# Rows of the next stage's input scattered by the two-expert stages, and one block for the start of the 64-wide attention, in an eight-stage kernel

## The chip, the cores and the metric

The kernel runs on one core of one Trainium2 chip. A core has TensorE (PE, matrix products), VectorE (DVE), ScalarE (ACT), GpSimd (POOL) and SyncE (SP, which here only issues DMAs), each with a queue of its own that is worked off in order; they meet through semaphores. DMAs issued by SyncE or GpSimd run on 16 shared DMA engines. The metric is the time of one execution in microseconds on the device; lower is better.

## The reference, cut to what matters

Input is x of 16 × 512 tokens of 128 floats. Eight layers follow, each with a layer norm ahead and a residual sum:

```python
x = x + attn_a(layernorm(x))          # 16 heads of 8, q and k through an rms norm
x = x + pair_ffn(layernorm(x))        # 8 experts, 2 chosen
x = x + attn_b(layernorm(x))          # 16 heads of 8, with a bias that decays with distance
x = x + pair_ffn(layernorm(x))
x = x + attn_relative(layernorm(x))   # 16 heads of 8, relative positions
x = x + choice_ffn(layernorm(x))      # each of 8 experts picks its tokens
x = x + attn_wide(layernorm(x))       # 16 heads of 64, q and k scaled to length 1
x = x + choice_ffn(layernorm(x))
```

The two layers that the change is about, in what they compute:

```python
def pair_ffn(x):                      # x is the normalised input
    gates = sinkhorn((x @ router_w + router_b) / max(temperature, 0.1), 3)
    vals, idx = top_k(gates, 2)
    g = relu(x @ wg[e]);  p = x @ wp[e]          # 128 -> 256, for every expert e
    out_e = (g * p) @ wo[e]                      # 256 -> 128
    return x + sum over the 2 of out_e * vals_e / (sum(vals) + 1e-8)

def attn_wide(x):
    q, k, v = x @ Wq.T, x @ Wk.T, x @ Wv.T       # 128 -> 16 heads of 64
    q = l2norm(q) * q_scale;  k = l2norm(k) * k_scale
    return softmax(q @ k.T / 8) @ v  @ Wo.T + bo
```

So a token leaves a two-expert layer as x + xn + y, with xn the normalised x and y the weighted results of its two experts.

## The kernel before

X, all 8192 tokens, stays in SBUF as [128, 64, 128] floats (4 MB): 16 batches of 512 tokens, four tiles of 128 tokens each. `model()` calls eight stages: narrow_attention ("rms"), pair_feed_forward (top2_a, whose tiles print as `_top_a`), decay_attention ("decay"), pair_feed_forward (top2_b), narrow_attention ("relative"), choice_feed_forward (choice_a), wide_attention ("wide") and choice_feed_forward (choice_b). Every stage consists of one or two blocks; a block has a program for each engine, and no engine enters the next block before all have left this one.

**pair_feed_forward** (L2544). SyncE loads the weights. TensorE turns X and scores it against the router; the normalised tokens `xn` are made in halves: batches 0 to 7 by GpSimd, two instructions of 128x512 each (subtract L2882, multiply L2884), batches 8 to 15 by VectorE, one instruction per tile (L2935, 32 in all). VectorE goes on with the router's chain (L2939 and below), which ends in lists: `from_row`, which token stands in which row of which block, and `to_row`, to which row of the result it goes. There are 91 blocks of 128 rows, each for one pair of experts. SyncE stores `xn` with the token's two gates, 130 floats a token, as `xn_rows` in DRAM (L2687, 4 DMAs). GpSimd then issues all the traffic of the expert loop: `gather(k)` (L2888) reads 128 rows of `xn_rows` into a ring of 12 buffers `xg`, `scatter(k)` (L2894) writes the block's 128 result rows `yg` to `y_rows`; 12 gathers go ahead, then it is scatter, gather, scatter, gather. Rows of a block that belong to no token go to dump rows behind. A block on TensorE is 25 matmuls; VectorE multiplies the halves (`hidden`), copies the higher expert's weights (`bring_higher`) and adds the weighted two results (`both_parts`, L3078) into `yg`. In blocks 12 to 27 VectorE also adds `xn` to X (L3065, 16 instructions of 128x512). After the last scatter SyncE waits until all have landed, reads `y_rows` back in 4 DMAs of 1 MB (L2694), and VectorE adds it to X (L3113, 16 instructions).

**choice_feed_forward** (choice_a) does it otherwise: its scatters accumulate into `x_mid` in DRAM (L3273), and the stage behind loads X from there.

**The attention stages.** In the first stage, "rms", X comes from the input: SyncE issues the first batch's tiles (L591), the setup loads (L593), the second batch's (L595) and the other 14 (L598), and VectorE waits on x_first, x_second and x_rest at its first use of each. The stages decay and relative find X in SBUF; there SyncE issues only setup loads (L1763, L593), and later `no_shift` (L1771, L601), in relative also the bias rows (L604, L608), and then the stores of each batch's q and k parts to scratch (L1844, L662). Before those it clears the semaphores of the stage before.

**wide_attention** (L3541). A first block loads X's tiles and all weights; TensorE transposes 32 squares of 128x128 in eight groups (L3626: groups 0 to 3 are Wq and Wk, 4 and 5 Wv, 6 and 7 Wo), ScalarE copies each group (L3639), and TensorE and ScalarE bring the scales (L3630, L3641). A second block does the attention, whose order is a schedule of steps that every engine walks through. For the first batch it is: layer norm, TURN_X (L3748, transposes of xn), then for t = 0 to 3 QK (L3756, four products of 512 columns, which go through the two banks of `bench`), SQUARES (copy L3843 and square L3846 by ScalarE, sums L3915 by VectorE), ROOT (L3922), LNEXP (L3852, L3854) and NORM (L3930); then seven TURNs (L3774, transposes of q and k, copies by ScalarE). Then come the scores S (L3787), exponentials (L3888), sums (L3936), V (L3764) and the products with v for batch 0, into which the same steps for batch 1 are woven.

## Time and profile before

| | us |
|---|---|
| median of 3 runs | 5938.82 (5938.35 to 5939.02) |
| the profiled execution | 5937.41 |
| its span in the trace | 5935.6 |
| TensorE busy | 4886.7 (82%) |
| VectorE busy | 3676.8 (62%) |
| ScalarE busy | 3305.6 (56%) |
| GpSimd busy | 1501.5 (25%) |

The mean granted clock of TensorE is 0.906 of full speed. The 64-wide attention lies between 3672 and some 5535 us of the trace, the two two-expert stages between 668 and 1103 and between 2081 and 2516. The shares are means over eight stages with different limits; what a stretch is bound by is read from the windows and the order of events in it. Times in the rows are in us from the span's start. A row of the timeline gives start, length, engine and line, output and inputs, shapes and a count, and in brackets the idle time of the engine before it and what ended it.

### The profile page before, as it was taken

How to read it: one execution, taken by the hardware profiler on the slowest of the kernel's cores; microseconds unless marked ns; L12 is line 12 of the kernel's file. 1: busy time of each engine (PE TensorE's matmuls, PEld its weight loads, DVE VectorE, ACT ScalarE, POOL GpSimd, SP SyncE). 2: the span in 40 equal slices, each digit the busy share in tenths (PEclk: the TensorE clock that was granted, in tenths of full speed). 3: DMA queues.
4: the chain of work that ended last, by engine and by line, in shares of the span. 5: the costliest groups of instructions: out<-in, count | busy, mean ns of one | idle time of the engine just before them, and what ended most of it. 6: DMA issues, size and time to landing. Idle time of an engine off the chain costs nothing. (4 is left out here: it accounts for less than half of the span.)

```text
span 5935.6 us, 94648 instructions
## 1 busy us (share of the span) xinstructions
PE 4886.7 (82%) x30116; PEld 2539.8 (43%) x30212; DVE 3676.8 (62%) x7406; ACT 3305.6 (56%) x5224; POOL 1501.5 (25%) x1452
## 2 busy tenths in 40 slices
PE   6999769389888859758888476899999999999557
PEld 2222469334444449712222354343343343343445
DVE  5444564577777785467777761667667666666671
ACT  5999525345555515448888022656666656666113
POOL 1111137324334217623322175000000000000157
PEclk8999779689999959979999577999999999999678
DMA  3222122313333221223222224000000000000213
GB/s 81 64 64 64 40 53 50 81 54 89 88 96 92 74 52 48 68 60 66 58 55 49 66 45 78 1 0 0 0 0 0 0 0 0 0 0 0 66 30 49
DMA packets 227987, 264.41 MB, mean 45 GB/s; under 512 B 36842, under 2 KB 194378, under 8 KB 221320
## 3 DMA queue, kind: packets, MB, share of 16 engines
q1 hardware_dynamic: 184276, 194.33, 12.5%
q0 software_dynamic: 43392, 66.05, 6.2%
q8 instruction: 173, 2.83, 0.2%
q14 instruction: 146, 1.20, 0.1%
HBM read 163.33 MB, written 96.12 MB: 44 GB/s over the span
## 5 line engine op out<-in xcount | busy, mean ns | idle before, releaser
L3888 ACT ACTIVATE prob_wide<-slot_wide 128x1024 f32<-128x1024 f32 x512 | 494.0, 1016 | 149.7 <-PE slot_wide L3787 149.7
L2172 ACT ACTIVATE prob_decay<-slot_decay 128x640 f32<-128x640 f32 x512 | 359.0, 706 | 342.6 <-PE slot_decay L2019 341.5
L996 ACT ACTIVATE prob_rms<-slot_rms 128x1024 f32<-128x1024 f32 x512 | 503.7, 1088 | 57.6 <-PE slot_rms L839 55.4
L2506 DVE TENSOR_TENSOR slot_decay<-slot_decay,dtab_decay 128x512 f32<-128x512 f32 (+3 forms) x1024 | 454.1, 493 | 128.6 <-PE slot_decay L1998 101.8
L996 ACT ACTIVATE prob_relative<-slot_relative 128x1024 f32<-128x1024 f32 x512 | 497.6, 1046 | 48.0 <-PE slot_relative L839 46.5
L3787 PE MATMUL slot_wide<-qT_wide,kT_wide 64*128 64x512 f32 x2048 | 508.8, 615 | 2.9 <-ACT prob_wide L3888 2.9
L3253 POOL TENSOR_TENSOR xn_choice_b<-X,stats_choice_b 128x512 f32<-128x512 f32 x8 | 8.4, 1047 | 1892.6 <-DVEq L3435 1892.6
L1361 DVE TENSOR_TENSOR prob_relative<-prob_relative,rtab_relative 128x1024 f32<-128x1024 f32 (+1 forms) x256 | 394.3, 1546 | 130.8 <-ACT prob_relative L996 122.7
L3800 PE MATMUL obank_wide<-prob_wide,v_wide 128*64 128x512 f32 x2048 | 467.7, 598 | 1.8 <-DVE zT_wide L3950 1.8
L3936 DVE TENSOR_TENSOR sums_wide<-sums_wide,prob_wide 128x1024 f32<-128x1024 f32 x256 | 313.6, 1225 | 28.7 <-ACT prob_wide L3888 0.2
L863 PE MATMUL obank_relative<-prob_relative,vaug_relative 128*32 128x512 f32 x2048 | 276.2, 612 | 39.5 <-DVE prob_relative L1361 38.0
L3861 ACT ACTIVATE rinv_wide<-rbank_wide 128x512 f32<-128x512 f32 x128 | 76.4, 597 | 409.5 <-PE rbank_wide L3811 409.5
L3756 PE MATMUL bench_wide<-wT_wide,xnT_wide 128*128 128x512 f32 x512 | 264.5, 639 | 44.9 <-ACT sq_wide L3846 25.4
L3787 PEld LDWEIGHTS slot_wide<-qT_wide,kT_wide 64*128 64x128 f32 x2048 | 176.0, 186 | 287.9 <-issue 280.9
L863 PE MATMUL obank_rms<-prob_rms,vaug_rms 128*32 128x512 f32 x2048 | 274.6, 608 | 2.7 <-ACT osb_rms L1005 1.9
L3800 PEld LDWEIGHTS obank_wide<-prob_wide,v_wide 128*64 128x64 f32 x2048 | 135.8, 136 | 318.0 <-issue 315.4
L3936 DVE TENSOR_TENSOR sums_wide<-prob_wide 128x1024 f32<-128x1024 f32 x128 | 156.8, 1225 | 174.2 <-ACT prob_wide L3888 174.2
L2013 PE MATMUL slot_decay<-qst_decay,kst_decay 128*128 128x512 bf16 (+3 forms) x992 | 219.2, 300 | 38.3 <-DVE slot_decay L2506 34.7
L3947 DVE TENSOR_TENSOR rfix_wide<-rbank_wide,rinv_wide 128x512 f32<-128x512 f32 x128 | 88.5, 692 | 247.5 <-ACT rinv_wide L3863 247.5
L1998 PE MATMUL slot_decay<-qst_decay,kin_decay 128*128 128x128 bf16 (+3 forms) x960 | 211.3, 297 | 33.2 <-ACT prob_decay L2172 14.5
L839 PE MATMUL slot_rms<-qst_rms,kst_rms 64*128 64x512 bf16 x1024 | 195.4, 390 | 35.0 <-DMA kst_rms<-scratch_rms 27.2
L839 PE MATMUL slot_relative<-qst_relative,kst_relative 64*128 64x512 bf16 x1024 | 192.7, 390 | 22.8 <-issue 17.3
(843 smaller groups left out, 10669.4 us busy)
## 6 DMA issues: line engine op xcount, KB each, us to landing
scratch_decay<-parts_decay SPq DMA_DIRECT2D x192, 128.0 KB, 2.4
qst_decay<-scratch_decay SPq DMA_DIRECT2D x128, 128.0 KB
scratch_rms<-parts_rms SPq DMA_DIRECT2D x96, 128.0 KB, 2.3
kst_rms<-scratch_rms POOLq DMA_DIRECT2D x96, 128.0 KB, 5.5
kst_decay<-scratch_decay SPq DMA_DIRECT2D x192, 64.0 KB
kin_decay<-scratch_decay SPq DMA_DIRECT2D x192, 64.0 KB
scratch_relative<-parts_relative SPq DMA_DIRECT2D x96, 128.0 KB, 2.4
kst_relative<-scratch_relative POOLq DMA_DIRECT2D x96, 128.0 KB, 6.3
```

The lines of the kernel that those rows point to most:

```text
L839: last = nc.tensor.matmul(slot[:, u % 3, k * S:k * S + m], kst[half_rows(k), buffer[0], pair, kb * P:(kb + 1) * P], qst[half_rows(k), buff ...
L863: last = nc.tensor.matmul(obank[32 * j:32 * j + 32, c0:c1], vaug[:, vp, kb, head(g, j), :], prob[:, Q % 2, j, at + c0 - q0:at + c1 - q0], ...
L996: nc.scalar.activation(prob[:, Q % 2, p:G:2, at:at + m], slot[:, u % 3].rearrange("p (k c) -> p k c", k=2)[:, :, 0:m], ACT.Exp).then_inc(e ...
L1361: last = nc.vector.tensor_tensor(v, v, of_group(rtab, g)[:, :, :, c0:c0 + (hi - lo) * P], ALU.mult)
L2013: last = nc.tensor.matmul(slot[:, u % 3, at:at + m], kst[:, h, kb * P:(kb + 1) * P], qst[:, h, q0:S], start=not decay, stop=not decay, ski ...
L2172: nc.scalar.activation(prob[:, Q % 2, j, 0:c1 - c0], slot[:, u % 3, c0:c1], ACT.Exp).then_inc(exp_done, 1)
L2506: last = nc.vector.tensor_tensor(sl, sl, dtab[:, h, 0:m], ALU.mult)
L3756: nc.tensor.matmul(bench[:, j % 2, :], xnT[:, t * P:(t + 1) * P], wT[:, j // 2, (j % 2) * S:(j % 2 + 1) * S], start=True, stop=True).then_ ...
L3787: last = nc.tensor.matmul(slot[:, u % 2, hh * S:(hh + 1) * S], kT[r, Q, kb * P:(kb + 1) * P], qT[r, Q, :], start=True, stop=True)
L3800: nc.tensor.matmul(obank[W * hh:W * hh + W, :], v[:, kb, (2 * Q + hh) * W:(2 * Q + hh + 1) * W], prob[:, Q % 2, kb, hh * S:(hh + 1) * S], ...
L3888: nc.scalar.activation(prob[:, Q % 2, u % 4, :], slot[:, u % 2, :], ACT.Exp).then_inc(exp_done, 1)
L3936: add = nc.vector.tensor_tensor(sums[:, Q % 2, :], first, prob[:, Q % 2, i + 1, :], ALU.add)
```

## The change

In the two-expert stages, the rows of `xn_rows` grow from 130 to 258 floats; the new 128 hold SUM = X + xn. GpSimd forms it in place in X, 16 additions of 128x512 behind its normalising instructions; SyncE stores it in 4 DMAs ahead of the 4 of `xn`. The gather brings it with the rest, VectorE adds it to the block's result in a second instruction, and the scatter writes whole rows of the next stage's input, `x_after_0` or `x_after_1`. The 16 additions in blocks 12 to 27, the read-back and its additions are gone. The stages decay and relative get X by DMA in the way that "rms" does.

In wide_attention the two blocks become one. The loads that the first products need (ident, Wq, Wk) have a semaphore of their own and go first. TensorE transposes groups 0 to 3, then X's tiles, then does QK, whose sixteen products go through six banks (two of `bench`, four of `slot`) in the first batch. Groups 4 to 7 and the scales follow as a step WEIGHTS behind QK 3. LNEXP and NORM of a tile come after the next tile's ROOT. Two of the seven TURNs stand before the first scores, two more behind the first two S, the other ones before V.

```diff
@@ pair_feed_forward: GpSimd @@
+                pool.wait_ge(xn_by_pool, BY_POOL)
+                for b in range(NB):
+                    at = slice(b * TPB, (b + 1) * TPB)
+                    pool.wait_ge(xT_filled, b + 1)
+                    if b >= BY_POOL:
+                        pool.wait_ge(xn_by_dve, b - BY_POOL + 1)
+                    nc.gpsimd.tensor_tensor(X[:, at], X[:, at], xn[:, at, 0:D], ALU.add).then_inc(x_summed, 1)
...
-                        y_rows, bass.IndirectOffsetOnAxis(ap=to_row[:, k:k + 1], axis=0), yg[:, k % RING, :],
+                        x_rows, bass.IndirectOffsetOnAxis(ap=to_row[:, k:k + 1], axis=0), yg[:, k % RING, :],
@@ pair_feed_forward: SyncE @@
+                out_rows = xn_rows.rearrange("(i p) c -> p i c", p=P)
+                for g in range(NB // GROUP):
+                    at = slice(g * GROUP * TPB, (g + 1) * GROUP * TPB)
+                    sp.wait_ge(x_summed, (g + 1) * GROUP)
+                    sp.dma_start(out_rows[:, at, SUM:CT], X[:, at]).then_inc(sums_stored, 16)
...
-                    sp.dma_start(out_rows[:, at], xn[:, at]).then_inc(xn_stored, 16)
-                sp.wait_ge(x_added, 1)
+                    sp.dma_start(out_rows[:, at, 0:C], xn[:, at]).then_inc(xn_stored, 16)
                 for u in range(RING):
                     sp.wait_ge(y_sent[u], 16 * rounds[u] * (turn + 1))
-                in_rows = y_rows[0:NB * S].rearrange("(i p) d -> p i d", p=P)
-                for g in range(NB // GROUP):
-                    at = slice(g * GROUP * TPB, (g + 1) * GROUP * TPB)
-                    sp.dma_start(back[:, at], in_rows[:, at]).then_inc(y_back[g], 16)
@@ pair_feed_forward: VectorE @@
-                    nc.vector.scalar_tensor_tensor(out=yg[:, k % RING, :], in0=ybank[:, k % 2, D:2 * D],
-                                                   scalar=xg[:, k % RING, GATES + 1:GATES + 2], in1=part[:, k % 2, :],
-                                                   op0=ALU.mult, op1=ALU.add).then_inc(yg_ready, 1)
+                    link(nc.vector.scalar_tensor_tensor(
+                        out=yg[:, k % RING, :], in0=ybank[:, k % 2, D:2 * D],
+                        scalar=xg[:, k % RING, GATES + 1:GATES + 2], in1=part[:, k % 2, :], op0=ALU.mult, op1=ALU.add))
+                    nc.vector.tensor_tensor(yg[:, k % RING, :], yg[:, k % RING, :], xg[:, k % RING, SUM:CT], ALU.add
+                                            ).then_inc(yg_ready, 1)
...
-                    if RING <= k < RING + NB:
-                        last = add_normalised(k - RING)
...
-                dve.wait_ge(x_added, 1)
-                for g in range(NB // GROUP):
-                    dve.wait_ge(y_back[g], 16)
-                    for b in range(g * GROUP, (g + 1) * GROUP):
-                        at = slice(b * TPB, (b + 1) * TPB)
-                        last = nc.vector.tensor_tensor(X[:, at], X[:, at], back[:, at], ALU.add)
@@ decay_attention, narrow_attention: SyncE @@
-                if rms:
+                if x_in is not None:
                     sp.dma_start(X[:, 0:TPB], x_in[:, 0:TPB]).then_inc(x_first, 16)
                 for dst, src in loads:
                     sp.dma_start(dst, src).then_inc(loaded, 16)
-                if rms:
+                if x_in is not None:
                     sp.dma_start(X[:, TPB:2 * TPB], x_in[:, TPB:2 * TPB]).then_inc(x_second, 16)
@@ wide_attention: the first batch's schedule @@
                 yield "QK", t
                 yield "SQUARES", t
                 yield "ROOT", t
-                yield "LNEXP", t
-                yield "NORM", t
-            for c in range(C - 1):
+                if t:
+                    yield "LNEXP", t - 1
+                    yield "NORM", t - 1
+            yield "WEIGHTS",
+            yield "LNEXP", TPB - 1
+            yield "NORM", TPB - 1
+            for c in range(FIRST_TURNS):
                 yield "TURN", c, 1
@@ wide_attention: TensorE @@
+                        if at_start(b, -1) and t == 0:
+                            pe.wait_ge(setup_act, 4)
                         for j in range(4):
-                            bench_free(j % 2)
-                            nc.tensor.matmul(bench[:, j % 2, :], xnT[:, t * P:(t + 1) * P],
+                            i = (4 * t + j) % 6 if at_start(b, -1) else j % 2
+                            bench_free(i)
+                            nc.tensor.matmul(qk_bank(b, 4 * t + j), xnT[:, t * P:(t + 1) * P],
...
+                pe.wait_ge(first_loaded, 16 * len(first_loads))
+                for m in range(4):
+                    turn_weights(m)
                 walk(pe, do)
```

What GpSimd has in a row between its last normalising instructions and the expert loop, in top2_a, before:

```order
63 L2882 TENSOR_TENSOR xng_top_a<-X,stats_top_a 128x4x128
64 L2884 TENSOR_TENSOR xng_top_a<-xng_top_a,stats_top_a 128x4x128
65 L2888 DMA xg_top_a<-xn_rows_top_a,from_row_top_a 128x130 x12
66 L2894 DMA y_rows_top_a<-yg_top_a,to_row_top_a 19840x128
67 L2888 DMA xg_top_a<-xn_rows_top_a,from_row_top_a 128x130
```

and now:

```order
64 L2888 TENSOR_TENSOR xng_top_a<-xng_top_a,stats_top_a 128x4x128
65 L2896 TENSOR_TENSOR X<-X,xng_top_a 128x512 x16
66 L2899 DMA xg_top_a<-xn_rows_top_a,from_row_top_a 128x258 x12
67 L2905 DMA x_after<-yg_top_a,to_row_top_a 19840x128
68 L2899 DMA xg_top_a<-xn_rows_top_a,from_row_top_a 128x258
```

Sixteen additions stand between the normalising and the first twelve gathers; the rest keeps its order, with wider rows and another target.

SyncE from the last weights of top2_a (`down`) to decay's first store to scratch (ISA rows are the clears of semaphores), before:

```order
80 L2678 DMA down_top_a<-in_L_ffn_wo 128x2x128 x8
81 L142 ISA x71
82 L2687 DMA xn_rows_top_a<-xng_top_a 128x16x130 x4
83 L2694 DMA xng_top_a<-y_rows_top_a 128x16x128 x4
84 L2672 UNCONDITIONAL_BRANCH
85 L1758 UNCONDITIONAL_BRANCH
86 L1763 DMA ident_decay<-in_consts 128x128
...
99 L1763 DMA nega_decay<-in_consts 128x128
100 L142 ISA x43
101 L1771 DMA no_shift_decay<-qst_decay 3x8192
102 L1844 DMA scratch_decay<-parts_decay 16x8x512 x6
```

and now:

```order
81 L143 ISA x71
82 L2690 DMA xn_rows_top_a<-X 128x16x128 x4
83 L2696 DMA xn_rows_top_a<-xng_top_a 128x16x130 x4
84 L2677 UNCONDITIONAL_BRANCH
85 L1761 UNCONDITIONAL_BRANCH
86 L1764 DMA X<-x_after 128x4x128
87 L1766 DMA ident_decay<-in_consts 128x128
...
100 L1766 DMA nega_decay<-in_consts 128x128
101 L1768 DMA X<-x_after 128x4x128
102 L1771 DMA X<-x_after 128x4x128 x14
103 L143 ISA x40
104 L1774 DMA no_shift_decay<-qst_decay 3x8192
105 L1847 DMA scratch_decay<-parts_decay 16x8x512 x6
```

The four reads of results are gone, four stores of sums stand ahead of those of `xn`, and 16 loads of X stand around decay's setup loads, ahead of the clears and the stores to scratch.

TensorE from the block change ahead of the 64-wide attention to the scores of its first batch (`prob` holds the raw weights there), before:

```order
6121 L3618 UNCONDITIONAL_BRANCH
6122 L3626 MATMUL bench_wide<-ident_wide,prob_wide 128x128 x32
6123 L3630 MATMUL obank_wide<-ident_wide,scales_wide 128x8
6124 L3604 UNCONDITIONAL_BRANCH
6125 L3731 UNCONDITIONAL_BRANCH
6126 L3748 MATMUL bench_wide<-ident_wide,xn_wide 128x128 x4
6127 L3756 MATMUL bench_wide<-wT_wide,xnT_wide 128x512 x16
6128 L3774 MATMUL bench_wide<-ident_wide,qk_wide 128x128 x56
6129 L3787 MATMUL slot_wide<-qT_wide,kT_wide 128x512 x8
```

and now:

```order
6122 L3727 MATMUL bench_wide<-ident_wide,prob_wide 128x128 x16
6123 L3743 MATMUL bench_wide<-ident_wide,xn_wide 128x128 x4
6124 L3754 MATMUL bench_wide<-wT_wide,xnT_wide 128x512 x2
6125 L3754 MATMUL slot_wide<-wT_wide,xnT_wide 128x512 x4
...
6129 L3754 MATMUL slot_wide<-wT_wide,xnT_wide 128x512 x2
6130 L3727 MATMUL bench_wide<-ident_wide,prob_wide 128x128 x16
6131 L3763 MATMUL obank_wide<-ident_wide,scales_wide 128x8
6132 L3780 MATMUL bench_wide<-ident_wide,qk_wide 128x128 x16
6133 L3793 MATMUL slot_wide<-qT_wide,kT_wide 128x512 x4
```

Half of the weights' transposes and the scales moved behind the sixteen QK products, the change of blocks is gone, and 16 of the 56 transposes of q and k are done before the first scores.

## Rows read from the trace of the kernel before

**Rows 1.** Windows: length, busy us (instructions) of each engine, granted clock, DMA share, GB/s.

```profile
900.00:950.00 50.00, 50.00 (x450) 50.00 (x450) 24.11 (x56) 27.36 (x73) 39.22 (x36) 1.00 0.21 50
```

**Rows 2.** Timeline: start, length, engine, line; the end of top2_a.

```profile
1080.13 0.35 DVE L3078 SCALAR_TENSOR_TENSOR yg_top_a<-ybank_top_a,xg_top_a,part_top_a 128x128 f32<-128x128 f32 x1 [1.41 <-ACT part_top_a L2845]
1080.76 0.96 POOL L2894 DMA_INDIRECT y_rows_top_a<-yg_top_a,to_row_top_a  x1 [0.80 <-DVE yg_top_a L3078]
1083.83 9.86 SPq L2694 DMA_DIRECT2D xng_top_a<-y_rows_top_a  x4
...
1103.93 0.35 SPq L1763 DMA_DIRECT2D ident_decay<-in_consts  x1
```

**Rows 3.** Timeline: the end of top2_b.

```profile
2493.85 0.97 POOL L2894 DMA_INDIRECT y_rows_top_b<-yg_top_b,to_row_top_b  x1 [0.79 <-DVE yg_top_b L3078]
...
2516.76 0.36 SPq L593 DMA_DIRECT2D ident_relative<-in_consts  x1
```

**Rows 4.** Timeline: the end of choice_a.

```profile
3666.25 1.55 POOL L3273 DMA_INDIRECT x_mid<-yg_choice_a,ids_choice_a  x1 [0.30 <-issue]
3672.01 0.37 SPq L3608 DMA_DIRECT2D X<-x_mid  x1
```

**Rows 5.** Timeline of 697 to 724: normalising in top2_a.

```profile
701.00 19.49 DVE L2935 TENSOR_SCALAR xng_top_a<-X,stats_top_a 128x128 f32<-128x128 f32 x32
701.95 1.05 POOL L2884 TENSOR_TENSOR xng_top_a<-xng_top_a,stats_top_a 128x512 f32<-128x512 f32 x1
702.95 1.05 POOL L2882 TENSOR_TENSOR xng_top_a<-X,stats_top_a 128x512 f32<-128x512 f32 x1
714.75 1.05 POOL L2884 TENSOR_TENSOR xng_top_a<-xng_top_a,stats_top_a 128x512 f32<-128x512 f32 x1
720.41 0.68 DVE L2939 TENSOR_TENSOR shift_top_a<-ybank_top_a,shift_top_a 128x512 f32<-128x512 f32 x1
```

**Rows 6.** Timeline of 714 to 721: VectorE there.

```profile
713.67 6.82 DVE L2935 TENSOR_SCALAR xng_top_a<-X,stats_top_a 128x128 f32<-128x128 f32 x20
```

**Rows 7.** Timeline of 850 to 870: GpSimd and VectorE in the expert loop.

```profile
860.93 1.21 POOL L2894 DMA_INDIRECT y_rows_top_a<-yg_top_a,to_row_top_a  x1 [0.30 <-issue]
861.46 0.68 DVE L3065 TENSOR_TENSOR X<-X,xng_top_a 128x512 f32<-128x512 f32 x1
862.45 0.97 POOL L2888 DMA_INDIRECT xg_top_a<-xn_rows_top_a,from_row_top_a  x1 [0.30 <-issue]
```

**Rows 8.** Timeline: SyncE at the start of the first stage.

```profile
5.63 13.59 SPq L598 DMA_DIRECT2D X<-in_L_attn_a_x  x14
```

**Rows 9.** Timeline: the start of decay.

```profile
1115.59 0.23 DVE L2298 TENSOR_SCALAR bqkv_t_decay<-bqkv_t_decay 128x128 f32<-128x128 f32 x1 [11.43 <-DMA nega_decay<-in_consts]
1141.05 3.85 SPq L1844 DMA_DIRECT2D scratch_decay<-parts_decay  x6
```

**Rows 10.** Timeline: the start of relative, SyncE's store and TensorE's first use of bias rows.

```profile
2544.43 3.83 SPq L662 DMA_DIRECT2D scratch_relative<-parts_relative  x6
2560.02 7.71 PE L813 MATMUL slot_relative<-prob_relative,rev_relative 128*128 128x384 f32 x16
```

**Rows 11.** Timeline: the start of the 64-wide attention.

```profile
3684.87 6.89 PE L3626 MATMUL bench_wide<-ident_wide,prob_wide 128*128 128x128 f32 x32 [27.58 <-DMA prob_wide<-in_L_attn_b_Wv]
3696.06 0.87 DVE L191 BATCH_NORM_STATS2 stats_wide<-X 128x6 f32<-128x128 f32 x4 [10.86 <-PEq L3604]
3701.57 1.11 PE L3748 MATMUL bench_wide<-ident_wide,xn_wide 128*128 128x128 f32 x4 [9.65 <-DVE xn_wide L203]
3703.45 6.05 PE L3756 MATMUL bench_wide<-wT_wide,xnT_wide 128*128 128x512 f32 x8 [0.77 <-ACT xnT_wide L3834]
3718.92 0.18 DVE L3922 TENSOR_SCALAR ss_wide<-ss_wide 128x32 f32<-128x32 f32 x1
3720.34 2.29 DVE L3930 TENSOR_TENSOR qk_wide<-qk_wide,ss_wide 128x2048 f32<-128x2048 f32 x1
3735.17 4.37 PE L3774 MATMUL bench_wide<-ident_wide,qk_wide 128*128 128x128 f32 x20 [6.17 <-DVE qk_wide L3930]
```

184 lines of the change are left out of this document (102 added, 82 removed).

## The prediction

> **What bounds the kernel now.** The kernel runs eight stages one after the other, each in blocks that all engines leave together, so I read it by stage: first the busy time of the engines in a window of each kind of work, then, in order of time, the few microseconds around every place that the diff touches. In the expert loop of the two-expert stages TensorE works in 50.00 of 50 us [rows 1]; its 450 matmuls are 18 blocks of 25, 2.78 us each, and the other engines fit beside it. The loop's speed is TensorE's. What the change can give or cost lies outside it, in stretches where TensorE sits idle: the end of a stage, the start of the next, the router before the expert loop, and the first batch of the 64-wide attention.
>
> **End of the two-expert stages: gain.** After the last scatter of top2_a is issued at 1080.76, SyncE waits for it to land, reads 4 MB back with 4 DMAs, VectorE adds, and the next stage's first DMA goes out at 1103.93: 23.17 us [rows 2]. In top2_b it is 2493.85 to 2516.76, 22.91 us [rows 3]. The change drops the read-back and the adds. What is left is what choice_a has already, whose scatters go straight to the next stage's input: 3666.25 to 3672.01, 5.76 us from the last scatter's issue to the next stage's first DMA [rows 4]. Its scatter takes 1.55 us to issue where the pair stage's takes 0.96 [rows 2, 4], so I subtract 0.6 and a little for landing (SyncE's first read at 1083.83 is 3.07 after the issue, which is issue, landing and wake-up) and take 5.2; bounds 4.6, which is those 3.07 and some 1.5 of block change, and 5.8. Each block now has a second VectorE instruction before its scatter; for the last block it lies on the path, and its 128x128 neighbour takes 0.35 [rows 2]: +0.3. So each tail shrinks to 5.5: 23.17 − 5.5 = 17.7 and 22.91 − 5.5 = 17.4, together **−35** (−33 to −37).
>
> **GpSimd's new adds: cost.** GpSimd gets 16 adds of 128x512 right behind its 16 normalising instructions. They look free, since GpSimd then waits for the router and the first gather anyway. They are not, by the profile. While GpSimd runs its instructions of 1.05 us, VectorE's own 128x128 normalising instructions come one to each of GpSimd's: from 701.00 to 713.67 twelve of the 32 are done, 1.06 us each [rows 5, 6]. GpSimd's last one ends at 714.75 + 1.05 = 715.80; the 18 that are left by then (two more went between) are done by 720.41, 0.26 us each [rows 5, 6]. VectorE alone would take 0.26 for one that takes 1.06 beside GpSimd, and what follows it at 720.41, the router's first step, begins at once: it was waiting for VectorE, and the whole router up to the first gather is VectorE's chain. With 16 more GpSimd instructions of some 1.06 us, VectorE does 16 of its 18 at that pace and the last two at its own: 16 × (1.06 − 0.26) = **+12.8 a stage, +25.6** in both. Bounds: 0, if an add of X and xn doesn't hold VectorE; 16 × 1.06 = +17 a stage if VectorE gets nothing while they run. Behind each wait of GpSimd (transposes of X done, VectorE's normalised batches) stand only these adds and the gathers, which come 100 us later. SyncE's four stores of the sums, 4 MB, have from there to the router's end, and are hidden.
>
> **Gathers, scatters and the second VectorE instruction in the loop: nothing.** A gather is issued in 0.97 us, a scatter in 1.21, 0.30 of gap behind each: 2.78 us for a block of 2.78 [rows 1, 7]. GpSimd is full to the last tenth. The gather's rows grow from 520 to 1032 bytes, the number of rows stays; I take issue as unchanged, since a descriptor is written for each row and not for each byte, and 0.2 us more landing for the first gather of each stage, **+0.4**. The 16 adds of 0.68 us on VectorE (k = 12 to 27) vanish and 91 of some 0.3 come; VectorE is busy 24 of 50 us there [rows 1, 7]. By itself: 0.
>
> Here a rule speaks against the change. The rows show a scatter of 1.21 us beside an add with two SBUF inputs, the 0.68 one at 861.46 [rows 7]. In the window from 900, where these adds are over, GpSimd's 36 instructions take 39.22 us, 1.09 each, which is the mean of 1.21 and 0.97 again [rows 1]: the add made nothing longer. A scatter beside nothing takes 0.96 [rows 2], so 0.25 is what some neighbour costs it. The Trainium skill, page "SBUF — State Buffer", calls the port pair that VectorE and GpSimd share an exclusive lock, also for a VectorE instruction with two SBUF inputs against a GpSimd one that reads SBUF, and warns that descriptors written by GpSimd starve behind it. By that, each block's new add could hold a scatter or a gather once; by the row, it doesn't, and the sum goes by the row. The rule's result is rival 4.
>
> **Start of decay and relative.** X now arrives by DMA: one DMA ahead of the setup loads and 15 behind. In decay VectorE waits for the last setup load until 1115.59, and one more DMA ahead moves that by its issue, **+0.5** (0.4 as for the others in the queue, to 3.7 if its data delays theirs) [rows 9]. The 14 X loads took 13.59 us of SyncE in the first stage [rows 8]; decay's setup loads have landed by 1115.59, so 1115.6 + 1.0 for the two single ones + 13.6 = 1130.2 in old time, 11 us before its first store to scratch at 1141.05 [rows 9]: hidden. Counted in the same way from relative's first DMA, 11.7 + 14.6 = 26.3 us after 2516.76 [rows 3], SyncE is free at about 2543 for its store at 2544.43, and the bias rows that it brings behind the X loads are read only at 2560.02 [rows 10]: 0, with 1.5 us of slack, so 0 to +3.
>
> **64-wide attention: gain.** Before, all weights (2.5 MB with X's first tiles) land, TensorE starts at 3684.87, transposes all eight groups in 6.89 us; a block change follows, VectorE's layer norm runs 3696.06 to 3701.57, and the first QK product starts at 3703.45 [rows 11]. Now TensorE starts on the first 1.37 MB (X, ident, Wq, Wk). At the rate of before, 2.5 MB in 12.9 us, that is 7.1 us, so about 3680 (3679 to 3682). Four groups take 3.45, the layer norm lies beside, and from X's transposes to QK it is 3703.45 − 3701.57 = 1.9, with 0.4 for the last copy: 3685.8, **−17.7** (−15 to −19). From QK's start to the first query transposes took 3735.17 − 3703.45 = 31.7 us. With six banks and the normalisation one tile later, the link from 3718.92 to 3720.34, 1.42 us in which VectorE mostly waits for ScalarE, can be hidden in three rounds: between 0 and 4.3; VectorE still has its own short instructions of it, so **−2.6**. The other four weight groups go into the 6.17 us in which TensorE waits for the last normalisation, and fit. Turning Q and K in two pieces is the same work in another order: 0, −3 to +1. Together **−20.3**.
>
> **The sum.** −35.1 + 25.6 + 0.4 + 0.5 − 20.3 = −28.9. The profiled execution took 5937.41 us: 5908.5. The median of the three runs is 1.4 above it, so 5909.9, and I say 5910.
>
> **Rivals.**
> 1. GpSimd's adds don't hold VectorE: −25.6 more, 5884. For it: these adds read X and xn without a broadcast operand; against: both of GpSimd's present instructions show the same 1.06 step [rows 5].
> 2. The adds hold VectorE altogether: 17 in place of 12.8 a stage, +8.4, 5918.
> 3. The 64-wide start gives only part: VectorE's and ScalarE's chain of squares, roots and normalisation sets the pace whatever the banks, and the first loads share the DMA rings with those behind: +4 to +9, 5914 to 5919. For it: TensorE already waits 6.17 us for VectorE there [rows 11].
> 4. The new VectorE add holds GpSimd once in a block: 2.78 + 0.25 against 2.78 is 0.25 a block, 79 blocks, 20 us of lag. The ring of 12 blocks takes up most, GpSimd catches up at the end where it only scatters; some 5 us a stage stay: 5920. The page's rule named above would do this; against it stands the row at 861.46.
> 5. Slower than before: the gather of 1032-byte rows takes longer to issue. GpSimd has no reserve. A lag of L a block grows over 79 blocks; the ring and the 12 last blocks hide about 31 us, so it shows from L = 0.39 us. An indirect DMA with more to do per row can be longer, 1.55 against 0.96 [rows 2, 4]. With the gather at twice 0.97 it is 79 × 0.97 − 31 = 46 a stage: 6002. From L = 0.58 (15 us a stage, the whole forecast gain) the kernel is slower than before. Against it: the count of rows is the same.
> 6. Relative's start comes late: SyncE's X loads go past the store to scratch, +3 to +10: 5913 to 5920.
>
> **How the numbers follow.** Forecast as summed, 5900 to 5914: 0.40. Rival 1: 0.14. Rivals 2, 3, 4 and 6, which all end between 5912 and 5926: 0.30 in all. Rival 5: 0.06. The rest, 0.10, is several of these at once or something unseen, half of it within 0.2% of before. The range takes the first three: **5880 to 5926**. A measurement of this kernel tells about 0.2% from no change, which is 5927 to 5951: faster 0.88, same 0.07, slower 0.05.
>
> **What would show it.** In the profile after: the last scatter's issue to the next stage's first DMA, 5.5 us, twice. VectorE's normalising instructions: a pitch of 1.06 until GpSimd's 32nd instruction, the router's first step at some 733; if at 720, rival 1. The block pitch in the loop at 2.78, gathers at 0.97, scatters at 1.21; if gathers are longer, rival 5, and TensorE's busy share there drops below full. The first QK product of the 64-wide stage 13.8 us after the stage's first DMA (31.4 before), and from there to the first turn 29 us. The store to scratch in relative 27.7 us after that stage's first DMA, as before. The forecast is wrong above all if VectorE's wait in the router stretch isn't GpSimd's doing.

## The result

| | before | changed |
|---|---|---|
| median, us (7 runs each) | 5938.35 (5933.46 to 5942.37) | 5917.13 (5913.61 to 5920.98) |
| profiled execution, us | 5937.41 | 5917.13 |
| its span, us | 5935.6 | 5915.0 |

The ratio is 0.9964, with a 95% interval of 0.9954 to 0.9974: the kernel became 21 us faster. The forecast was 29 us faster (5910, 5880 to 5926). Direction and range hold; the way there does not hold in every term.

The first DMA of each stage cuts both traces into stages. The first DMAs are at 668.01, 1103.93, 2081.24, 2516.76, 3266.65, 3672.01 and 5531.63 before, and at 665.62, 1101.12, 2077.05, 2513.78, 3265.10, 3671.28 and 5511.55 in the changed kernel.

| stage | before, us | changed, us | difference |
|---|---|---|---|
| rms (not changed) | 668.0 | 665.6 | −2.4 |
| top2_a | 435.9 | 435.5 | −0.4 |
| decay | 977.3 | 975.9 | −1.4 |
| top2_b | 435.5 | 436.7 | +1.2 |
| relative | 749.9 | 751.3 | +1.4 |
| choice_a (not changed) | 405.4 | 406.2 | +0.8 |
| wide | 1859.6 | 1840.3 | −19.3 |
| choice_b (not changed) | 404.0 | 403.5 | −0.5 |

The stages that the diff doesn't touch move by up to 2.4 us between these two executions, and over all traces of this case the first stage, the same in every kernel, takes 662.1 to 668.0 us. So a difference of a few us in a whole stage says nothing; where less is claimed below, it is read inside the stage. What remains is the 64-wide stage, which carries the whole gain, and the two-expert stages, which come out even.

### The profile page after: what moved, and what is told of

Read it like the earlier page. It is cut to its first block and busy times, and to the rows that moved or that the text cites. A ratio compares the mean times of both kernels' runs of the same rounds, so it can differ in the third digit from the quotient of the medians.

```text
span 5915.0 us, 94826 instructions
## 1 busy us (share of the span) xinstructions
PE 4881.9 (83%) x30116; PEld 2541.1 (43%) x30212; DVE 3720.4 (63%) x7524; ACT 3304.6 (56%) x5224; POOL 1537.2 (26%) x1484
## 5 line engine op out<-in xcount | busy, mean ns | idle before, releaser
L3907 ACT ACTIVATE prob_wide<-slot_wide 128x1024 f32<-128x1024 f32 x512 | 494.0, 1016 | 150.6 <-PE slot_wide L3793 150.6
L3754 PE MATMUL bench_wide<-wT_wide,xnT_wide 128*128 128x512 f32 x492 | 252.2, 634 | 39.1 <-ACT sq_wide L3859 19.6
```

The source lines that it names most:

```text
L3754: nc.tensor.matmul(qk_bank(b, 4 * t + j), xnT[:, t * P:(t + 1) * P], wT[:, j // 2, (j % 2) * S:(j % 2 + 1) * S], start=True, stop=True).th ...
L3907: nc.scalar.activation(prob[:, Q % 2, u % 4, :], slot[:, u % 2, :], ACT.Exp).then_inc(exp_done, 1)
```

## The profile after

First the page's line of busy time. VectorE has 118 instructions more (in each two-expert stage 91 new ones, and 32 gone), GpSimd 32 more; TensorE has the same number.

```profile
PE 4881.9 (83%) x30116; PEld 2541.1 (43%) x30212; DVE 3720.4 (63%) x7524; ACT 3304.6 (56%) x5224; POOL 1537.2 (26%) x1484
```

The timeline of the changed kernel where the normalised tokens of top2_a are made, with the first step of the router and the first gather (start, length, engine and line), answers to [rows 5]:

```profile
698.62 32.79 DVE L2947 TENSOR_SCALAR xng_top_a<-X,stats_top_a 128x128 f32<-128x128 f32 x32
...
713.50 15.91 POOL L2896 TENSOR_TENSOR X<-X,xng_top_a 128x512 f32<-128x512 f32 x14
...
731.34 0.68 DVE L2951 TENSOR_TENSOR shift_top_a<-ybank_top_a,shift_top_a 128x512 f32<-128x512 f32 x1
732.05 1.24 DVE L2953 TENSOR_TENSOR shift_top_a<-shift_top_a,parts_top_a 128x512 f32<-128x512 f32 x1
...
830.16 1.07 POOL L2899 DMA_INDIRECT xg_top_a<-xn_rows_top_a,from_row_top_a  x1 [97.42 <-DVE from_row_top_a L3068]
```

VectorE's 32 instructions took 19.49 us before and take 32.79 now: 13.3 us more, with 12.8 in the forecast. A window of 714 to 720 was enough before to see VectorE go fast once GpSimd was through; now fourteen of GpSimd's adds follow each other without a pause, 15.91 us for the fourteen, and VectorE has no such stretch. An add takes 1.18 us at the median and comes every 1.14 us, where the forecast had 1.06 for both. The last add still makes one step of the router 1.24 us instead of 0.69. From the stage's first DMA the first gather comes after 830.16 − 665.62 = 164.5 us; before it was 818.68 − 668.01 = 150.7, by this row of the kernel before:

```profile
818.68 1.07 POOL L2888 DMA_INDIRECT xg_top_a<-xn_rows_top_a,from_row_top_a  x1 [102.88 <-DVE from_row_top_a L3056]
```

In the expert loop nothing moved. The window of the changed kernel that answers to [rows 1], then gathers and scatters by line (shortest, median and longest in ns, first and last start):

```profile
900.00:950.00 50.00, 50.00 (x451) 50.00 (x450) 28.18 (x73) 27.36 (x73) 39.23 (x36) 1.00 0.27 73
```

```profile
L2899 POOL DMA_INDIRECT xg_top_a<-xn_rows_top_a,from_row_top_a x91: 949/973/1071, 830.2 to 1063.3; - x91
L2905 POOL DMA_INDIRECT x_after<-yg_top_a,to_row_top_a x91: 968/1206/1212, 845.5 to 1092.3; - x91
```

TensorE is busy throughout, GpSimd's 36 instructions take 39.23 us as before (39.22), VectorE 28.18 instead of 24.11. The gather of 1032-byte rows is issued in 0.973 us. From first gather to last scatter the stage takes 262.2 us, before 262.1.

The end of top2_a in the changed kernel, and that of top2_b behind it, against [rows 2, 3]:

```profile
1091.77 0.29 DVE L3089 TENSOR_TENSOR yg_top_a<-yg_top_a,xg_top_a 128x128 f32<-128x128 f32 x1
1092.34 0.97 POOL L2905 DMA_INDIRECT x_after<-yg_top_a,to_row_top_a  x1 [0.82 <-DVE yg_top_a L3089]
1101.12 0.36 SPq L1764 DMA_DIRECT2D X<-x_after  x1
...
1101.19 3.51 POOL L2197 MEMSET vaug_decay<- 128x4096 f32 x1 [7.88 <-POOLq L2677]
...
2504.99 0.97 POOL L2905 DMA_INDIRECT x_after<-yg_top_b,to_row_top_b  x1 [0.82 <-DVE yg_top_b L3089]
2513.78 0.36 SPq L592 DMA_DIRECT2D X<-x_after  x1
```

From the last scatter's issue to the next stage's first DMA it is 8.78 and 8.79 us, 3.3 us more than the 5.5 of the forecast. Of the 5.5, 0.3 was for VectorE's second instruction, which lies ahead of the scatter (the row at 1091.77, 0.29 us); the distance itself was forecast as 5.2. Something in these 8.8 us isn't the scatter.

The start of the 64-wide stage, against [rows 11]: the stage's first DMA, TensorE's first transposes, X's transposes, the first QK product, the first turn, the first scores.

```profile
3671.28 0.38 SPq L3702 DMA_DIRECT2D X<-x_mid  x1
...
3678.63 3.76 PE L3727 MATMUL bench_wide<-ident_wide,prob_wide 128*128 128x128 f32 x16 [22.08 <-DMA prob_wide<-in_L_attn_b_Wk]
...
3682.31 1.09 PE L3743 MATMUL bench_wide<-ident_wide,xn_wide 128*128 128x128 f32 x4
...
3684.16 3.75 PE L3754 MATMUL bench_wide<-wT_wide,xnT_wide 128*128 128x512 f32 x4 [0.77 <-ACT xnT_wide L3847]
...
3712.91 3.86 PE L3780 MATMUL bench_wide<-ident_wide,qk_wide 128*128 128x128 f32 x16 [6.08 <-DVE qk_wide L3958]
...
3716.71 3.01 PE L3793 MATMUL slot_wide<-qT_wide,kT_wide 64*128 64x512 f32 x8
```

QK starts 12.9 us after the stage's first DMA instead of 31.4, and the first turn comes 28.75 us later instead of 31.72. That is 21.5 us; the stage as a whole gains 19.3. How much of this is the change and how much the two executions is taken up with the experiments.

## The experiments

**Which part brings what.** Two kernels, each with one half of the change: in the first the function of the 64-wide stage is the new one and all others are those of before; in the second it is the other way round.

```diff
@@ wide_alone, against the kernel before @@
-def wide_attention(...):    # of the kernel before
+def wide_attention(...):    # of the changed kernel
```

> The kernel before with the new 64-wide stage alone; the two-expert stages, decay and relative are as before. From the stage starts of the two traces (1859.6 us of the 64-wide stage before, 1840.3 after) the theory 'all of the net gain is the 64-wide start' expects 19 us less than before: about 5919, ratio 0.9967. The rival 'the two-expert stages bring part of the 21 us' expects a smaller gain here, 10 to 15 us: 5923 to 5928.

Measured: 5911.74 us against 5934.19, ratio 0.9963 (0.9949 to 0.9977), 22 us less where 19 were expected. The 64-wide part alone gives the gain of the whole change.

```diff
@@ pair_alone, against the changed kernel @@
-def wide_attention(...):    # of the changed kernel
+def wide_attention(...):    # of the kernel before
```

> The changed two-expert stages, decay and relative, with the 64-wide stage of before. If the dropped read-back (14 us less from last scatter to next stage) is given back by the router stretch that GpSimd's adds lengthen (13 to 15 us more), this is within 3 us of before: 5936 to 5941. The rival, that the two-expert part gained what I forecast, 4.5 us a stage, expects 5929.

Measured: 5936.22 us, ratio 1.000 (0.9991 to 1.001). The two-expert part costs as much as it gives, as the first case has it; my forecast of 4.5 us a stage doesn't stand. The interval is some 6 us wide to either side, so the 9 us of the forecast for both stages lie outside it.

**GpSimd's adds, later.** They wait until VectorE has made its last normalised batch.

```diff
@@ adds_late, against the changed kernel: GpSimd @@
                 pool.wait_ge(xn_by_pool, BY_POOL)
+                pool.wait_ge(xn_by_dve, NB - BY_POOL)
                 for b in range(NB):
                     at = slice(b * TPB, (b + 1) * TPB)
                     pool.wait_ge(xT_filled, b + 1)
-                    if b >= BY_POOL:
-                        pool.wait_ge(xn_by_dve, b - BY_POOL + 1)
```

> The changed kernel, but GpSimd starts its 16 adds only when VectorE has made its last normalised batch. Theory 'GpSimd's adds held VectorE's normalising instructions': these are back to 19.5 us from 32.8, so the router's first step comes 13 us earlier in each two-expert stage; the adds now lie beside the router's own VectorE instructions and lengthen some of them (in the changed kernel the 16th add made one of them 1.24 us instead of 0.69), 16 x 0.5 = 8 us at most of the 13 given back. Expected 5 to 13 us a stage less than the changed kernel: 5891 to 5907. Rival 'the normalising is slow for another cause' (SBUF traffic of the matmuls, the stores of sums): no change of its 32.8 us, 5917.

Measured: 5893.01 us, ratio 0.9927 (0.991 to 0.9943). The two-expert stages take 425.6 and 426.1 us by their first DMAs, 10 less than in the changed kernel. The timeline of this kernel, VectorE's normalising, GpSimd's adds behind it and some of the router's steps beside them:

```profile
697.51 19.48 DVE L2946 TENSOR_SCALAR xng_top_a<-X,stats_top_a 128x128 f32<-128x128 f32 x32
716.90 0.68 DVE L2950 TENSOR_TENSOR shift_top_a<-ybank_top_a,shift_top_a 128x512 f32<-128x512 f32 x1
717.12 21.09 POOL L2895 TENSOR_TENSOR X<-X,xng_top_a 128x512 f32<-128x512 f32 x16 [4.83 <-issue]
717.62 1.23 DVE L2952 TENSOR_TENSOR shift_top_a<-shift_top_a,parts_top_a 128x512 f32<-128x512 f32 x1
718.88 1.55 DVE L2953 TENSOR_TENSOR gate_top_a<-shift_top_a,rb_top_a 128x512 f32<-128x512 f32 x1
720.47 0.69 DVE L2965 TENSOR_REDUCE tok_top_a<-gate_top_a 128x64 f32<-128x512 f32 x1
```

The normalising is back at 19.48 us. The adds now hold the router's steps instead: two take 1.23 and 1.55 us, where the same step without GpSimd beside it is 0.69; the reduction at 720.47, which has one input, keeps its 0.69, and so do the copies from PSUM. The adds take 1.18 us at the median here too, as in the changed kernel, but up to 1.64, and 21.09 in all. Held work is cheaper there: only some of VectorE's steps are hit, VectorE waits for other engines in between, and of the 13.3 us given back 9.8 are left at the first gather (819.15 − 664.45 = 154.7 us after the stage's first DMA, against 164.5).

**The sums without GpSimd.** x + (x − m)·r is x·(1 + r) − m·r, one ScalarE instruction a tile with a scale and a bias for each token.

```diff
@@ adds_act, against the changed kernel: ScalarE (GpSimd's 16 adds are gone) @@
+                def add_normalised(b):
+                    act.wait_ge(stats_ready, 2)
+                    act.wait_ge(xT_filled, b + 1)
...
+                    for t in range(b * TPB, (b + 1) * TPB):
+                        last = nc.scalar.activation(X[:, t, :], X[:, t, :], ACT.Identity, bias=stats[:, t, 11:12],
+                                                    scale=stats[:, t, 10:11])
+                    last.then_inc(x_summed, 1)
@@ behind the copies of batches 12 to 15, and two batches behind each logarithm of the three rounds @@
+                    add_normalised(4 + 4 * i)
+                    add_normalised(5 + 4 * i)
@@ VectorE, behind the statistics @@
+                link(nc.vector.tensor_scalar(stats[:, :, 10], stats[:, :, 9], 1.0, None, ALU.add))
+                nc.vector.scalar_tensor_tensor(out=stats[:, :, 11], in0=stats[:, :, 6], scalar=-1.0,
+                                               in1=stats[:, :, 9], op0=ALU.mult, op1=ALU.mult).then_inc(stats_ready, 1)
```

> The changed kernel, but ScalarE makes the sums, tile by tile, as X times (1 + r) minus m times r, four batches between its copies and twelve in the pauses of the router; GpSimd's 16 adds are gone. Theory 'whatever GpSimd does in SBUF holds VectorE, on whichever side of the normalising it lies': VectorE's normalising takes 19.5 us and the router's instructions their old lengths, so the first gather comes 150.7 us after the stage's start as in the kernel before (164.6 in the changed one, about 155 with the late adds): 14 us a stage less than the changed kernel, 5889, some 4 below the late adds. Rival 'ScalarE's extra work comes in front of the router's exponentials': 64 instructions of 0.35 us, of which a third lies in the way: 5 to 10 us a stage given back, 5895 to 5905.

Measured: 5891.72 us, ratio 0.9925 (0.9908 to 0.9942). The two-expert stages take 422.5 and 423.1 us, 13 to 14 less than in the changed kernel, with 14 expected. Its timeline:

```profile
699.20 18.63 DVE L2961 TENSOR_SCALAR xng_top_a<-X,stats_top_a 128x128 f32<-128x128 f32 x32
717.75 0.67 DVE L2965 TENSOR_TENSOR shift_top_a<-ybank_top_a,shift_top_a 128x512 f32<-128x512 f32 x1
718.46 0.69 DVE L2967 TENSOR_TENSOR shift_top_a<-shift_top_a,parts_top_a 128x512 f32<-128x512 f32 x1
...
722.74 0.26 ACT L2838 ACTIVATE tok_top_a<-tok_top_a 128x64 f32<-128x64 f32 x1 [0.75 <-DVE tok_top_a L2983]
722.90 3.17 ACT L2823 ACTIVATE X<-X,stats_top_a 128x128 f32<-128x128 f32 x8
```

VectorE's instructions beside ScalarE's sums have their own lengths, and eight sums fit into a pause of the router. Yet the total is only 1.3 us below the late adds, which is inside both intervals. In the profiled execution, the slowest of the four, relative took 762 us, 10 above the others. That is taken up below.

**What GpSimd must do to hold VectorE.** The kernel above, with 16 memsets on GpSimd where the adds had been.

```diff
@@ gp_memset, against adds_act: GpSimd @@
+                for b in range(NB):
+                    last = nc.gpsimd.memset(xg[:, 2 * (b % 6):2 * (b % 6) + 2, 0:256], 0.0)
+                    if b % 6 == 5 or b == NB - 1:
+                        link(last)
```

> The kernel whose sums ScalarE makes, with 16 memsets of 128x512 on GpSimd where its 16 adds stood in the changed kernel: GpSimd only writes SBUF there and reads nothing. With the sums on ScalarE VectorE's 32 normalising instructions took 18.6 us. Theory 'VectorE's normalising instruction is held by any GpSimd instruction on SBUF': one VectorE instruction comes to each memset, at a pitch of the memset's own 0.45 us or so instead of 0.26, so 16 x 0.2 = some 3 us more, 21 to 23 us. Rival 'only GpSimd instructions that read SBUF hold it': 18.6 us as without them.

Its timeline, the two rows of the stretch:

```profile
699.51 22.11 DVE L2965 TENSOR_SCALAR xng_top_a<-X,stats_top_a 128x128 f32<-128x128 f32 x32
713.12 8.96 POOL L2909 MEMSET xg_top_a<- 128x512 f32 x16
```

22.11 us in place of 18.63: 3.5 us more for memsets that read nothing; the kernel took 5900.51 us (one run). So for VectorE's normalising instruction, f32 from SBUF to SBUF, a GpSimd instruction that only writes SBUF counts too. The Trainium skill, page "SBUF — State Buffer", section "Who interferes with whom", says the same: a VectorE instruction in a 2-port mode and a GpSimd instruction exclude each other for the whole instruction, while for a VectorE instruction with two SBUF inputs only a GpSimd one that reads SBUF counts. The first half agrees with 22.11 against 18.63, though no row names the mode in which the normalising instruction ran; for the second the late adds, which read, lengthened the two-input steps to 1.23 and 1.55 us, and no run here set a writing GpSimd instruction beside one.

**Who is late at the end of the two-expert stage.** Three kernels move or lengthen one engine's end.

```diff
@@ tail_dve, against the changed kernel: SyncE, then VectorE @@
-                for u in range(RING):
-                    sp.wait_ge(y_sent[u], 16 * rounds[u] * (turn + 1))
...
                 dve.wait_ge(yg_ready, BLOCKS)
+                for u in range(RING):
+                    dve.wait_ge(y_sent[u], 16 * rounds[u] * (turn + 1))
+                nc.vector.memset(col[:, 7:8], 0.0).then_inc(x_summed, 1)
+                dve.wait_ge(x_summed, NB + 1)
```

> The changed kernel, but at the end of the two-expert stages VectorE instead of SyncE waits for the scatters and then clears one column, which dates their landing in the trace. In the changed kernel 8.8 us pass from the last scatter's issue to the next stage's first DMA, 3.3 more than forecast. Theory 'SyncE is slow from its last wait to leaving the block': VectorE's mark comes 3 us after the scatter's issue and the next stage's first DMA 0.5 us later, as in the kernel before, where VectorE was the last to leave: 5 us a stage less, 5907. Rival 'GpSimd is the late one, it leaves the block late after its last indirect DMA': the mark at 3 us, but the next stage again at 8.8 us, no change of time. Third: the scatters land late, the mark itself comes at 8 us, no change of time.

The end of its top2_a: the last scatter, VectorE's mark, the next stage.

```profile
1093.17 0.97 POOL L2903 DMA_INDIRECT x_after<-yg_top_a,to_row_top_a  x1 [0.82 <-DVE yg_top_a L3087]
1096.41 0.06 DVE L3115 MEMSET col_top_a<- 128x1 f32 x1 [3.52 <-DMA x_after<-yg_top_a,to_row_top_a]
1101.95 0.36 SPq L1764 DMA_DIRECT2D X<-x_after  x1
```

The scatter has landed 3.2 us after its issue, as forecast, and 5.5 us later the next stage still hasn't begun; 8.78 us in all, and 5914.97 us for the kernel, ratio 0.9965 (0.9951 to 0.9979). It isn't SyncE and isn't the landing. My first theory falls.

```diff
@@ pe_pad, against the changed kernel: TensorE, behind the last block @@
                 fall(BLOCKS - 1)
+                pe.wait_ge(yg_ready, BLOCKS)
+                for j in range(12):
+                    nc.tensor.matmul(gbank[:, j % 2, :], ident[:], relu[:, 0, :], start=True, stop=True,
+                                     skip_group_check=True)
```

> The changed kernel with 12 more matmuls of 128x512 on TensorE after the last block of each two-expert stage, whose result nobody reads; they start when the last result rows are made and take some 7 us. Theory 'TensorE is the one that leaves the block late, some 10 us after its last instruction': the next stage's first DMA moves from 8.8 to some 17 us after the last scatter's issue. Rival 'GpSimd is the late one': TensorE's end, some 7 us after the scatter's issue, is still hidden, and the 8.8 us stay.

```profile
1088.94 10.57 PE L2812 MATMUL gbank_top_a<-relu_top_a,ident_top_a 128*128 128x512 f32 x24 [1.17 <-DVE yg_top_a L3093]
1089.16 0.96 POOL L2909 DMA_INDIRECT x_after<-yg_top_a,to_row_top_a  x1 [0.80 <-DVE yg_top_a L3093]
...
1099.76 0.36 SPq L1764 DMA_DIRECT2D X<-x_after  x1
```

The added matmuls, 12 in the program and 24 rows in the profile, took 10.57 us where I had planned 7, and end at 1099.51; the next stage starts 0.25 us later. Without them it would have started at 1089.16 + 8.78 = 1097.94. TensorE leaves the block in a quarter of a microsecond, so it isn't the late one.

```diff
@@ pool_mark, against the changed kernel: GpSimd, behind the last scatter (SyncE's waits are gone) @@
+                nc.gpsimd.memset(place[:, 0], 0.0).then_inc(x_summed, 1)
+                for u in range(RING):
+                    pool.wait_ge(y_sent[u], 16 * rounds[u] * (turn + 1))
+                nc.gpsimd.memset(place[:, 1], 0.0).then_inc(x_summed, 1)
+                pool.wait_ge(x_summed, NB + 2)
```

> The changed kernel, but GpSimd waits for the scatters in place of SyncE and writes one column before the wait and one behind it. Theory 'GpSimd leaves the block a fixed time, 7.8 us, after its last instruction': with its second mark at 3.3 us after the scatter's issue the next stage starts at about 11 us in place of 8.8. Rival 'what is slow is the clearing up after the indirect DMAs, counted from the DMA': the next stage stays at 8.8 us. Third, 'it is not GpSimd': 8.8 us as well, told from the second by the run with more matmuls.

```profile
1091.74 0.97 POOL L2903 DMA_INDIRECT x_after<-yg_top_a,to_row_top_a  x1 [0.79 <-DVE yg_top_a L3092]
1092.71 0.17 POOL L2917 MEMSET place_top_a<- 128x64 f32 x1
1094.53 0.15 POOL L2920 MEMSET place_top_a<- 128x64 f32 x1 [1.65 <-DMA x_after<-yg_top_a,to_row_top_a]
1102.69 0.36 SPq L1764 DMA_DIRECT2D X<-x_after  x1
```

The second mark ends at 1094.68 and the next stage starts at 1102.69, 8.0 us later and 10.95 after the scatter's issue. With the landing already over, the time still counts from GpSimd's last instruction; in top2_b of this kernel it is again 8.0 us. In the changed kernel it is 1101.12 − 1093.31 = 7.8 us. So GpSimd is the one that leaves late, and it takes 7.8 to 8.0 us after whatever it did last. The kernel before hid this: its GpSimd had 22 us of read-back in which to leave. In choice_a, from which I took the price, the same distance is 3672.01 − 3667.80 = 4.2 us [rows 4]. Why it is 7.8 in one stage and 4.2 in the other stays open. (The kernels of the last two experiments ran once, 5914.03 and 5917.86 us; what counts in them are the rows.)

**The 64-wide start, piece by piece.**

```diff
@@ two_banks, against the changed kernel @@
-            i = i % 6 if at_start(b, -1) else i % 2
+            i = i % 2
...
-                            i = (4 * t + j) % 6 if at_start(b, -1) else j % 2
+                            i = j % 2
```

> The changed kernel with the first batch's QK products in two banks as before; the later normalisation stays. In the changed kernel the first product to the first turn took 28.7 us, before 31.7. Theory 'the later normalisation brings it, since VectorE is what the rounds wait for': 28.7 to 29.5 here. Rival 'the six banks bring it': 31 to 32.

Its first QK product and its first turn:

```profile
3683.85 1.95 PE L3754 MATMUL bench_wide<-wT_wide,xnT_wide 128*128 128x512 f32 x4 [0.77 <-ACT xnT_wide L3847]
...
3711.98 3.87 PE L3780 MATMUL bench_wide<-ident_wide,qk_wide 128*128 128x128 f32 x16 [6.38 <-DVE qk_wide L3958]
```

28.13 us with two banks, 28.75 with six, 31.72 in the kernel before. By these three numbers the six banks bring nothing. But TensorE's granted clock was not the same in them. The first four us of QK in the changed kernel, in this one, and in wide_alone, which has the changed kernel's 64-wide stage, and below them wide_alone's first QK product and first turn:

```profile
3684.00:3688.00 4.00, 3.84 (x5) 1.81 (x6) 0.00 (x0) 1.15 (x4) 0.00 (x0) 0.50 1.18 291
```

```profile
3684.00:3688.00 4.00, 3.68 (x8) 1.09 (x8) 0.92 (x1) 2.78 (x6) 0.00 (x0) 1.00 1.21 290
```

```profile
3680.00:3684.00 4.00, 4.00 (x10) 1.71 (x9) 1.08 (x1) 3.18 (x7) 0.00 (x0) 1.00 1.20 294
```

```profile
3679.68 1.96 PE L3755 MATMUL bench_wide<-wT_wide,xnT_wide 128*128 128x512 f32 x4 [0.77 <-ACT xnT_wide L3848]
...
3706.74 3.60 PE L3781 MATMUL bench_wide<-ident_wide,qk_wide 128*128 128x128 f32 x16 [6.68 <-DVE qk_wide L3959]
```

The profiled execution of the changed kernel began QK at 0.50 of the clock, the lower level of 1.2 GHz; the other two had all of it. With six banks and the full clock it is 27.06 us, and the same to 0.02 us in all nine traces that have six banks and the full clock there. So the six banks bring 28.13 − 27.06 = 1.1 us, and the lower clock cost the changed kernel's trace 1.7. The kernel before began QK at 0.50 as well, so its 31.72 is fairly compared with 28.75: of these 3.0 us, some 1.9 are left for normalising a tile one round later, so that VectorE has a reduction to do while ScalarE takes logarithms. That is an estimate, since no run has two banks, the lag and the lower clock. Both ranges of the expectation were missed, and its theory holds in part only.

```diff
@@ turns7c, against the changed kernel @@
-    FIRST_TURNS = 2
+    FIRST_TURNS = 7
...
-                        for c in range(4, C - 1):
+                        for c in range(max(4, FIRST_TURNS), C - 1):
```

> The changed kernel with all seven turns of q and k before the first scores, as in the kernel before. From the first turn to the end of the 64-wide stage took 1796.5 us before and 1798.6 after. Theory 'turning in two pieces brings nothing, work is only moved, and the waits between ScalarE and TensorE cost 2 us': the stage takes 1837 to 1838 us instead of 1839.9. Rival 'the first exponentials come earlier and the end with them': 1842 to 1846.

The stage takes 1840.5 us from its second DMA to the next stage, in the changed kernel 1839.9. Neither range holds, and the question asked for less than executions of one kernel differ by. From the first turn to the next stage the kernel before took 1796.5 us and the changed one 1798.6, but pair_alone, with the old 64-wide stage, took 1798.8, and the eleven traces with the new one lie between 1796.1 and 1801.1. So there are no 2 us to be explained, and whether turning in two pieces helps by one or two us isn't shown. From first DMA to first DMA the old stage took 1859.6 and 1862.6 us in its traces, the new one 1836.5 to 1841.2. (two_banks and turns7c ran once, 5918.20 and 5916.84 us.)

**A candidate.** The sums on ScalarE and all seven turns ahead.

> Candidate: the changed kernel with the sums on ScalarE and all seven turns ahead of the first scores. The run with the sums on ScalarE gave 422.9 and 423.5 us for the two-expert stages against 435.9 and 437.2 in the changed kernel, but its relative stage took 10 us more than in the other runs. Theory 'that was this execution's clock and not the kernel': relative takes 751 us here and the whole 5917 - 27 - 1 = about 5889, in most executions 5880 to 5890. Rival 'the sums on ScalarE make relative slower': relative again at 761 and the whole at 5892 to 5895.

Measured: 5888.52 us (5 runs, 5887.01 to 5890.54), ratio 0.9923 (0.991 to 0.9937), the lowest median of all, 46 us below the kernel before in the same session; its interval overlaps those of adds_act and adds_late. (The expectation counts stages from the second DMA, which is 0.4 us later in decay and relative.) Its two-expert stages take 422.3 and 423.8 us from first DMA to first DMA. Its relative took 755.2 us, against 750 to 752.5 in the kernels whose sums are not on ScalarE, 762.1 in adds_act and 760.9 in gp_memset. So the rival was not refuted: three of three kernels with the sums on ScalarE have a slower relative, by 3 to 12 us. What is longer there stands in two rows each over the whole execution, VectorE's products with the relative table and TensorE's matmuls that wait for them (busy us, mean ns, idle time before), first of adds_late, then of adds_act:

```profile
L1364 DVE TENSOR_TENSOR prob_relative<-prob_relative,rtab_relative 128x1536 f32<-128x1536 f32 x128 | 225.6, 1763 | 74.3 <-ACT prob_relative L997 72.0
L864 PE MATMUL obank_relative<-prob_relative,vaug_relative 128*32 128x512 f32 x2048 | 276.9, 613 | 39.6 <-DVE prob_relative L1364 38.0
```

```profile
L1364 DVE TENSOR_TENSOR prob_relative<-prob_relative,rtab_relative 128x1536 f32<-128x1536 f32 x128 | 232.8, 1819 | 79.6 <-ACT prob_relative L997 77.5
L864 PE MATMUL obank_relative<-prob_relative,vaug_relative 128*32 128x512 f32 x2048 | 277.0, 613 | 45.4 <-DVE prob_relative L1364 43.8
```

The same 128 products take 232.8 us instead of 225.6. It is 232.8 in all three kernels with ScalarE's sums and 225.6 in the ten others, to 0.1 us. GpSimd's adds of 128x512 in that stage (sq_relative) go the other way, 1.97 us each instead of 2.67, and those of 128x256 take 1.34 instead of 0.76. So VectorE and GpSimd fall on each other's instructions in another pattern there, and TensorE waits 43.4 to 43.8 us for VectorE's products instead of 37.9 to 40.0. That tells 3 to 6 us of the loss. What sets the pattern, why it goes with the sums on ScalarE in the stages before, and what the rest of the loss is, stays open.

## Why the prediction was right, and where it was wrong

Range and direction were right, and by pair_alone and wide_alone both rest on the 64-wide start alone. Term by term:

- **GpSimd's adds, +12.8 a stage: right.** The normalising got 13.3 us longer, and the first gather comes 13.9 (top2_a) and 14.8 us (top2_b, 2242.47 − 2077.05 = 165.4 against 150.6) later. One more router step held by the last add gives 0.55 of the rest. The adds came every 1.14 us instead of 1.06. Rival 2, nothing for VectorE while they run, would have been 17. Rivals 1 and 2 are out. What made the term was to read VectorE's pace beside GpSimd and without it from two windows of the same 32 instructions [rows 5, 6].
- **The tails, −17.7 and −17.4: too large by 3.3 each.** They shrank from 23.17 and 22.91 to 8.8 us, not to 5.5: −14.4 and −14.1. The failed step is "what is left is what choice_a has already". I took choice_a's distance as landing and block change and made it smaller, because the pair stage's scatter is issued faster. What sets both is how long GpSimd takes to leave the block after its last instruction, 7.8 us here and 4.2 there. [rows 2] couldn't show it, since GpSimd had been idle for 22 us; only an engine that ends last shows its own price. I should have kept the upper bound open instead of closing it at 5.8.
- **Loop, gather, second VectorE instruction, 0: right.** The gather is 0.973 us against 0.969, the scatter 1.206 against 1.210, the loop 262.2 us against 262.1. Rivals 4 and 5 are out: VectorE and GpSimd do hold each other up in the normalising, but the new add, with two SBUF inputs, made no scatter longer. Rival 4 also asked more of the rule than its page states: by the Trainium skill, page "SBUF — State Buffer", section "Who interferes with whom", it was a VectorE copy that stalled DMAs issued by GpSimd, and a two-input instruction did not. The scatters agree, 1.206 us beside the adds against 1.210.
- **Starts of decay and relative, +0.5 and 0: −0.1 and 0, right within what can be told.** The first VectorE step on the setup came 11.58 us after decay's first DMA instead of 11.66, since 1112.70 − 1101.12 stands against [rows 9]. Relative's store to scratch came 27.67 us after its first DMA, exactly as before (2541.45 − 2513.78 against [rows 3, 10]). The stage took 751.3 us against 749.9, within what an unchanged stage moves.
- **The 64-wide start, −20.3: right, −19.3 in this pair of executions.** QK started 1 us earlier than forecast (12.9 us instead of 13.8 after the first DMA), most of it because TensorE began after 7.35 us and not after 8. From QK to the first turn it was 3.0 less instead of 2.6, both traces at the lower clock. The forecast gave all of it to six banks and lag together, and the runs divide it into some 1.1 and 1.9. That the whole stage gained 19.3 and not 21.5 is within what executions differ by; wide_alone gained 22. Rival 3 is out, and so is rival 6, by relative's 27.67. Over all traces, 1859.6 and 1862.6 us for the old stage and 1836.5 to 1841.2 for the new one, the gain is 18 to 26 us.

The sum: −35.1 for the tails became −28.5, +25.6 for the adds +28.7, −20.3 became −19.3. That makes −19 where the forecast had −29, and the measured difference is −21. The term that was mis-sized most is the tails, by 6.6 us in all; the range held because its upper bound was set by other rivals, which didn't come true. The changed two-expert stages are a gain of 14 us at the end, paid with 14 us at the start, and one line in the right place, a later start of the adds, brings 10 of them back in each.

## What to carry to other kernels

An engine that stands idle is not free when its instructions hold up the one on the critical path: before work is put on GpSimd, look at how VectorE's own instructions fare beside the GpSimd instructions that are there already, and put the work where VectorE waits or give it to ScalarE. The price of a wait that is to be removed hides other waits under it: read the next one from a place where the engine in question was the last to end, not from a similar stage. A change of several parts is best cut by the first DMA of each stage; two parts that cancel each other look like one part without effect. And before two stretches of some 30 us are compared, look at the granted clock in both: here it hid what the six banks bring.
